# Attention of layers 1 and 3 in a fused four-layer transformer: scores on four 32-row groups, keys not expanded, rotary partners by transfers

## The reference, cut to what matters

```python
# layer 1
qkv = h @ w_qkv + b_qkv
q = _rope(q.reshape(B, T, n_head, hd)); k = _rope(k.reshape(B, T, n_head, hd))
attn = softmax(einsum('bhqd,bhkd->bhqk', q, k) * (1.0 / np.sqrt(hd)))
out = einsum('bhqk,bhkd->bhqd', attn, v)
x = x + (out.reshape(B, T, C) @ w_ao + b_ao)
# _rope: o0 = x0*cos - x1*sin ; o1 = x1*cos + x0*sin   (x0, x1: even and odd features)
# layer 3: no _rope; padding mask of keys and queries; x = x + gate * (out @ proj_w.T + proj_b)
```

## Time and profile before

| | us |
|---|---|
| median of three runs | 2149.85 |
| the profiled execution, its own time | 2150.09 |
| span of the profile | 2148.3 |
| mean granted TensorE clock | 0.993 |
| PE, DVE, ACT, POOL busy | 2049.8, 1314.9, 987.4, 405.0 |

### The profile page before, as it was taken

One profiled execution on the slowest core, in us unless ns is written; L12 is line 12 of the kernel. 1 busy time (PEld: TensorE's weight loads), 2 busy tenths in 40 slices (PEclk: granted clock), 3 DMA queues, 4 the chain that ended last, 5 costly groups with the idle time before them and its releaser, 6 DMA issues.

```text
span 2148.3 us, 44435 instructions
## 1 busy us (share of the span) xinstructions
PE 2049.8 (95%) x15652; PEld 1670.8 (78%) x15652; DVE 1314.9 (61%) x2537; ACT 987.4 (46%) x1581; POOL 405.0 (19%) x381
## 2 busy tenths in 40 slices
PE   7999999999999999999999999998999999998998
PEld 6887887778777888877777777776888777787887
DVE  5856565767766565654444555456666677775664
ACT  3444555444444333334444444445444555454443
POOL 3632112223221010101111111112001222210000
PEclk9999999999999999999999999999999999999999
DMA  6000000000000000000000000000000000000000
GB/s 224 21 10 8 7 11 15 9 7 15 7 8 13 18 20 10 20 5 7 7 6 5 5 0 5 5 2 16 5 5 5 16 6 10 10 1 9 21 20 30
DMA packets 18405, 33.38 MB, mean 16 GB/s; under 512 B 1298, under 2 KB 12050, under 8 KB 17810
## 3 DMA queue, kind: packets, MB, share of 16 engines
q1 hardware_dynamic: 18322, 32.25, 4.7%
HBM read 28.06 MB, written 4.19 MB: 15 GB/s over the span
## 4 chain that ended last, share of the span: by engine, by line
PE 79%; DVE 9%; issue 7%; ACT 2%; POOL 2%; DMA 0%; DVEq 0%; SPq 0%; ACTq 0%; POOLq 0%
PE psum L591 21%; PE psum L593 20%; PE psum L592 19%; PE psum L688 4%; PE psum L701 3%; PE psum L633 2%; PE psum L720 2%; PE psum L786 2%; PE psum L734 2%; PE psum L677 1%; DVE xn L1093 1%; PE psum L526 1%; DVE h_lo L1114 1%; DVE pb L1169 1%; PE psum L685 1%
## 5 line engine op out<-in xcount | busy, mean ns | idle before, releaser
L591 PE MATMUL psum<-h_hi,w_lo 128*128 128x512 f32 x1120 | 463.4, 414 | 11.7 <-DVE h_lo L1114 6.3
L593 PE MATMUL psum<-h_hi,w_hi 128*128 128x512 f32 x1120 | 441.6, 394 | 0.0
L592 PE MATMUL psum<-h_lo,w_hi 128*128 128x512 f32 x1120 | 440.8, 394 | 0.0
L1221 DVE TENSOR_TENSOR hid_lo<-hid,hid_hi 128x512 fp32r<-128x512 f32 x256 | 194.0, 759 | 266.2 <-ACT hid_hi L967 265.9
L967 ACT ACTIVATE hid_hi<-hid 128x512 fp32r<-128x512 f32 x256 | 161.7, 632 | 223.1 <-PE psum L593 133.0
L591 PEld LDWEIGHTS psum<-h_hi,w_lo 128*128 128x128 f32 x1120 | 212.4, 190 | 62.4 <-issue 11.0
L593 PEld LDWEIGHTS psum<-h_hi,w_hi 128*128 128x128 f32 x1120 | 211.8, 189 | 49.5
L592 PEld LDWEIGHTS psum<-h_lo,w_hi 128*128 128x128 f32 x1120 | 212.6, 190 | 39.0
L1303 POOL TENSOR_TENSOR rstd<-ms,half_t 128x4 f32<-128x4 f32 x64 | 65.4, 1021 | 903.9 <-DVE ms L1088 485.1
L1166 DVE TENSOR_REDUCE mx<-psum 128x8 f32<-128x512 f32 x192 | 132.4, 690 | 160.0 <-PE psum L677 106.7
L962 ACT ACTIVATE hid<-psum,vec 128x512 f32<-128x512 f32 x192 | 131.8, 687 | 182.8 <-PE psum L593 166.9
(11 more groups left out here) (140 smaller groups left out, 3601.1 us busy)
## 6 DMA issues: line engine op xcount, KB each, us to landing
stage<-in_w_dram SPq DMA_DIRECT2D x24, 256.0 KB, 2.7
stage<-in_w_dram SPq DMA_DIRECT2D x8, 512.0 KB, 3.5
out_dram<-xres SPq DMA_DIRECT2D x8, 512.0 KB, 2.9
xres<-in_x_dram SPq DMA_DIRECT2D x1, 3584.0 KB, 18.4
modw_mod<-in_modw_dram SPq DMA_DIRECT2D x2, 1536.0 KB, 13.6
stage<-in_w_dram SPq DMA_DIRECT2D x8, 384.0 KB, 3.3
stage<-in_w_dram SPq DMA_DIRECT2D x8, 192.0 KB, 2.4
modw_film<-in_modw_dram SPq DMA_DIRECT2D x1, 1024.0 KB, 7.4
```

The costliest lines, as they stand in the source:

```text
L591: nc.tensor.matmul(dst, s_lo, m_hi, start=start and j == 0, stop=False)
L592: nc.tensor.matmul(dst, s_hi, m_lo, start=False, stop=False)
L593: ins = nc.tensor.matmul(dst, s_hi, m_hi, start=False, stop=stop and j == len(pairs) - 1)
L1221: nc.vector.tensor_tensor(hid_lo[:, slot, :], hid32[:, slot, :], hid_hi[:, slot, :].bitcast(F32), ALU.subtract).then_inc(sem["hid"], 1)
```

## The change

1. Scores, layers 1 and 3: the keys stand in `kk` as projected, [128 rows, 512], not expanded. For each sequence four products run on the 32-row groups r = 0..3, each with 128 stationary columns (`qb`) and 64 moving columns, into bank r of four banks. All steps use the same columns of these four banks, so that scores of a step wait for both `s_free`, that is for DVE's pass over the step before. The mask of layer 3 becomes four products of 128 columns.
2. Layer 1: q and k are projected once. ACT writes the rows with bias to `rows1`, two transfers issued by ACT (`q_swap`, `k_swap`) exchange even and odd partitions into `swapped`, DVE multiplies the projection by cos (after ACT's copy), POOL multiplies `swapped` by sin and adds (`q_rot`, `k_rot`). ACT's four copies of keys per projection are gone.
3. `merge`, `proj` and `back` (and `back` of the mlp phases) fill the A banks, two fills each, and free them in halves. The wide banks are left to `heads`, the turned weights and the mlp.
4. Layer 1's `norm` is ACT's, not DVE's.
5. `on` is a stage of its own, and the table has a new order. `UP_AFTER`, the place of the next mlp's first projections, moves too.

```diff
@@ order_of, layers 1 and 3
-        return mask(1, 0) + [own("scores", 0), prev("probs_t", 7), own("q", 1), own("q_out", 1), prev("pv", 6), own("share"),
-                own("scores", 1), own("probs_t", 0), own("v", 0), prev("pv", 7), own("v_out", 0), own("v", 1),
-                own("v_out", 1), nxt("stats"),
-                own("scores", 2), nxt("norm"), own("probs_t", 1), prev("merge"), own("k", 1), own("k_out", 1), own("pv", 0),
...
+        return ([own("scores", 0), prev("probs_t", 7), prev("on", 5)] + [own("mask", 1)] * masks +
+                [own("k_swap", 1), own("q_rot", 1)] * turned + [prev("pv", 6), own("v", 0), prev("pv", 7), own("v_out", 0),
+                 nxt("stats"),
+                 own("scores", 1), own("probs_t", 0), prev("on", 7)] + [own("k_rot", 1)] * turned +
+                [own("v", 1), own("v_out", 1), nxt("norm"), own("share"),
+                 own("scores", 2), own("probs_t", 1), prev("merge"), own("pv", 0), own("q_out", 1), nxt("turn"),
+                 own("scores", 3), own("probs_t", 2), prev("proj"), own("pv", 1), nxt("split"),
+                 own("scores", 4), own("probs_t", 3), own("on", 1), nxt("q", 0), own("pv", 2), prev("back")] +
...
+                [own("scores", 6), own("probs_t", 5), own("on", 3), own("pv", 4), nxt("q", 1), nxt("q_out", 0)] +
...
@@ PE, scores
-                        for g in range(2):
-                            ins = nc.tensor.matmul(dst.rearrange("p (r g k) -> p r g k", g=2, k=S)[:, :, g, :],
-                                                   qb[:, c, 2 * j + g, :, :].rearrange("p h q -> p (h q)"),
-                                                   kx[:, c, 2 * j + g, :, :], start=layer == 1, stop=layer == 1 or g == 1)
+                        wait_alone(pe, sem[f"s_free{1 - slot}"], n_at(f"s_free{1 - slot}", ph, b, (k + 1) // 2))
...
+                            for r in range(4):
+                                rows = slice(32 * r, 32 * r + 32)
+                                ins = nc.tensor.matmul(group_scores[:, r, g * S:(g + 1) * S],
+                                                       qb[rows, c, seq, :, :].rearrange("p h q -> p (h q)"),
+                                                       kk[rows, c, seq * S:(seq + 1) * S], start=layer == 1,
+                                                       stop=layer == 1 or g == 1)
@@ PE, merge
-                    for g in range(SEQ):
-                        ins = nc.tensor.transpose(wide[:, g // 4, (g % 4) * P:(g % 4 + 1) * P], on[:, g, :], ident)
-                    ins.then_inc(sem["w_full"], 1)
+                    for u in range(2):
+                        dst, full = fill_a(ph, s, k, b, u)
+                        for g in range(4):
+                            ins = nc.tensor.transpose(dst[:, g * P:(g + 1) * P], on[:, 4 * u + g, :], ident)
+                        ins.then_inc(full, 1)
@@ ACT, new: normalizing, and the rotary partners of layer 1
+                elif s == "norm" and PHASES[ph] == ("attn", 1):
+                    act.wait_ge(sem["rstd"], n_at("rstd", ph, b, 1))
+                    for t in range(TILES):
+                        ins = nc.scalar.activation(xn[:, t, :], xres[:, b * TILES + t, :], ACT.Copy, scale=rstd[:, t:t + 1])
+                    for odd in range(2):
+                        act.dma_start(swapped[odd:P:2, which, :],
+                                      rows1[1 - odd:P:2, which, :]).then_inc(sem[f"{name}_swapped"], 16)
@@ DVE, heads' outputs: own stage
-                elif s == "pv" and layer in (1, 3):
-                    if slot == 0:
-                        return
+                elif s == "on":
                     dve.wait_ge(sem["o_full"], n_at("o_full", ph, b, k + 1))
```

More of the change, by code:

```diff
@@ L102, in order_of @@
     if layer in (1, 3):
-        mask = (lambda c, off: [("mask", c, off)]) if layer == 3 else (lambda c, off: [])
-        return mask(1, 0) + [own("scores", 0), prev("probs_t", 7), own("q", 1), own("q_out", 1), prev("pv", 6), own("share"),
-                own("scores", 1), own("probs_t", 0), own("v", 0), prev("pv", 7), own("v_out", 0), own("v", 1),
-                own("v_out", 1), nxt("stats"),
-                own("scores", 2), nxt("norm"), own("probs_t", 1), prev("merge"), own("k", 1), own("k_out", 1), own("pv", 0),
[L108 to L112, removed]
+        masks = layer == 3
@@ L139, in fills_in @@
         return DC
+    if s in ("merge", "proj", "back") and (kind == "mlp" or layer in (1, 3)):
+        return 2
     if kind == "attn" and s in ("q", "k", "v"):
-        return 2 if layer == 1 and s != "v" else 1
+        return 1
     return 1 if kind == "attn" and layer == 2 and s == "probs_t" else 0
@@ L284, in build @@
         kk = place("kk", [P, DC, BLK], F32, free + 8192)
[L285 to L289, removed]
+        q32 = place("q32", [P, DC, BLK], F32, free + 12288)
+        vb = place("vb", [P, TILES, 2, 2 * PAIRS * HW], F32, free + 16384)
+        on = place("on", [P, SEQ, P], F32, free + 16384 + 8704)
+        rows1 = place("rows1", [P, 2, BLK], F32, rot_at)
+        swapped = place("swapped", [P, 2, BLK], F32, rot_at + 4096)
+        assert free + 16384 + 8704 + 4096 <= wb
         free3 = wa + 8 * 2048
@@ L620, in stage_of @@
                         pe.wait_ge(mod_dve, 6)
-                if is_first(b) and (s, k) in (("probs_t", 0), ("pv", 0), ("down", 0)):
+                if is_first(b) and (s, k) == ("down", 0):
                     pe.wait_ge(sem["x_done"], n_at("x_done", ph, 0, 1))
+                if is_first(b) and (s, k) == ("probs_t", 0) and layer in (1, 3):
+                    pe.wait_ge(sem["out_rows"], n_at("out_rows", ph, 0, 0))
+                if is_first(b) and (s, k) == ("up", 0):
+                    for sl in range(2):
+                        pe.wait_ge(sem[f"s_free{sl}"], n_at(f"s_free{sl}", ph, 0, 0))
                 if s == "split" and ph == 0 and is_first(b):
@@ L779, in stage_of @@
                     pe.wait_ge(sem["out_rows"], n_at("out_rows", ph, b, 2))
-                    if kind == "mlp":
-                        pe.wait_ge(sem["x_done"], n_at("x_done", ph, b, 1))
-                    dst = mlp_back if kind == "mlp" else wide
-                    for t in range(TILES):
-                        for m in range(DC):
-                            o = (t % 2) * D + m * P
-                            ins = nc.tensor.transpose(dst[:, t // 2, o:o + P], y[:, m, t * P:(t + 1) * P], ident)
-                    ins.then_inc(sem["back" if kind == "mlp" else "w_full"], 1)
+                    for u in range(2):
+                        if layer == 2 and kind == "attn":
+                            dst, full = wide[:, u, :], sem["w_full"]
+                        else:
+                            dst, full = fill_a(ph, s, k, b, u)
+                        for t in range(2):
+                            for m in range(DC):
+                                o, tile = t * D + m * P, 2 * u + t
+                                ins = nc.tensor.transpose(dst[:, o:o + P], y[:, m, tile * P:(tile + 1) * P], ident)
+                        if u == 1 or full is not sem["w_full"]:
+                            ins.then_inc(full, 1)
             pe.wait_ge(sem["x_done"], n_at("x_done", 0, 0, 1))
@@ L1232, in stage_of @@
                     for m in range(DC):
[L1233 to L1246 removed]
+                        src = wide[:, m, :]
```

267 lines of the change are left out of this document (151 added, 116 removed).

## The result

The changed kernel takes 2270.23 us (median of four runs, 2262.48 to 2273.02), the kernel before 2148.95: 1.0559 times as long, 95% interval 1.0530 to 1.0587. The forecast was +58 us, the measurement +121. The direction was right, the time lies above the range, which ended at 2256. One of the eight executions of on_early (experiment 1) took 3219.51 us at a mean granted clock of 0.555, where the other seven took 2148.70 to 2153.41; the ratios leave it out, and its cause isn't known.

What follows compares the result with a forecast made beforehand. PE was taken to bound both attention stages. New waits and clock loss less PE savings gave +2.3 us a block in layer 1 and +5.4 in layer 3; 7.5 x 7.7 = +58 on 2150.09 gave 2208 us, range 2142 to 2256.

Steps and rivals of the forecast that it cites:

- Work taken off PE: Projections and scores on PE: 5.5 and 2.1 us a block saved in layer 1, 2.7 in layer 3.
- the change of tile shape: Score groups on PE: 0.14 us added to 0.46 for switching tile shape, giving 0.6 us in layer 1.
- The waits behind: PE's pv 4, 6 and 2 wait for VectorE's `on`: 2.9, 3.2, 0.9 us in layer 1; 2 x 2.3 + 0.9 in layer 3.
- Merge and turn in the projection banks: Turn waits until ScalarE and VectorE have read the merge: 3.6 us a block in layer 1, 2.4 in layer 3.
- h: Projection of q waits for h_lo: 1.3 us a block in layer 1, 0.6 in layer 3.
- Transfers hidden: Rotary transfers in layer 1: key ready 6.3 us after its projection, PE needs 9.5 us to scores 0, so no cost.
- The clock: Layers 1 and 3: one low-clock stretch in every second block, costing 0.8 us a block.
- the ends of the stages: Ramp and end of each attention stage count as a half block less, giving the factor 7.5 on the per-block change.
- Rival (c): Clock falls more than once a block in layers 1 and 3: 36 us more, 2244 us; chance 0.25.
- The range: Whole kernel: 2142 to 2256 us, leaving out rivals of total chance 0.15.

Runs made afterwards that it cites:

- on_early, experiment 1: Changed kernel with each `on` moved right behind the product it divides, ahead of the next pass over the scores; 2152.55 us, 1.0017 times the kernel before.
- added_wide: on_early with two products of 512 columns added ahead of each group of scores in layers 1 and 3; 2165.84 us, 1.0086 times the kernel before.
- experiment 2, before_on_late: Kernel before with only `on` moved late, behind the pass of a later segment; 2241.54 us, 1.0441 times the kernel before.
- Experiments 4 to 6: Changed kernel with scores over all 128 rows, 2454.99 us; on_early with score products made twice, 2191.42 us, or with two 512-column products per score group, 2165.84 us.
- one_wide: on_early with stages reordered per layer, plus one unread 512-column product ahead of every score group in layers 1 and 3; 2148.75 us, 1.0000 times the kernel before.
- held: on_early with stages reordered per layer, plus unread products (10 of 224 columns, 4 of 512) in two waits a block; 2121.82 us, 0.9885 times the kernel before.
- full_rows: Changed kernel with each of the eight score products of a group taken over all 128 rows in place of 32; 2454.99 us, 1.1436 times the kernel before.
- experiment 3: Changed kernel with unread products filling PE's waits before the fourth and sixth weight-times-value products and before turn; 2203.61 us, 1.0265 times the kernel before.

## Why the prediction was wrong, by its steps

- *Work taken off PE*: right. A group of scores takes 0.60 us in layer 1 from its start to the turns (525.85 to 526.45), the value taken between the bounds 0.3 and 1.84; taking the row groups away gave 1.83, the upper bound. That it was met to the digit is in part luck, since the 0.14 for the change of tile shape had no row behind it. In layer 3 it takes 0.62 with the mask, where the forecast had 0.75: 3.8 us saved a block for 2.7. The whole saving can be had from added_wide, whose clock is full: its span is 14.5 us over before, with 59 us of added products, 34 us more idle time and 2 us more lost to the clock, so about 80 us were saved; the forecast had 7.5 x 10.3 = 77, and with layer 3's 3.8 it is 85.
- *The waits behind* `on`: right. 7.0 us a block in layer 1 (2.9 + 3.2 + 0.9 = 7.0 forecast), 5.0 in layer 3 (5.5). Their cause is shown by experiment 1, and by 2 from the other side.
- *Merge and turn in the projection banks*: 3.2 us (3.6) and 1.9 (2.4), a little less than said. *h*: 1.3 and 0.7 (1.3 and 0.6).
- *Transfers hidden*: nothing speaks against it. They land after 2.1 us, and none of the 2.0 us that all score groups waited in the whole execution was for the rotary sums:

```profile
L706 PE MATMUL psum<-kk,qb 32*128 32x64 f32 x2048 | 94.9, 307 | 2.0 <-DVEq L1216 1.1 <-issue 0.9
```

- *The clock*: this term failed, by its size. It was 0.8 us a block in both layers. The sum without the clock, with the measured waits and scores, is 38.66 + 11.5 - 1.95 - 7.6 = 40.6 us in layer 1 and 33.25 + 7.6 - 1.2 - 3.8 = 35.85 in layer 3. The measured 49.0 and 40.9 leave 8.4 and 5.0 us. The trace bears this out directly: over the six periods the stretches at 0.50 add up to 17.6 and 8.5 us a block, of which 1.3 and 0.0 fall on waits; half of the rest, 8.2 and 4.3 us, is the work that they cost (the mean clocks of the windows allow 8.8 and 4.9). So the clock took about 8 and 4 to 5 us a block where the forecast had 0.8. Without any clock loss the sums give 7.5 x (1.1 + 2.6) = 28 us over the kernel before; most of the +121 is the clock. Put into the forecast, 8.4 and 5.0 for 0.8 each are 7.5 x (7.6 + 4.2) = +88 us on 2208; the smaller waits and layer 3's quicker scores take back 7.5 x (0.4 + 2.0) = 18: 2278. The four executions took 2262 to 2273; whether the ends of the stages, counted as half a block, make up the difference isn't shown.
- *Rival (c)*, with 2244 us, had the right mechanism at 0.25, and its price was too low as well, for the same reason. I counted stretches by the one in the earlier trace rows, 3.4 us long, and took 1.6 us for each. Here they were up to 10.24 us long inside the blocks, and three a block in layer 1. The error was to carry a price per wait over from a kernel whose work between the waits was wide. The change narrowed that work itself (256-column scores became 64-column ones, and in layer 1 24 products of 512 columns went), so each wait cost more clock than before: experiment 2, with waits of up to 2.2 us beside the old work, had 48 us of low time, on_early 120 with less idle time. The Trainium skill (TensorE: Matmul & The Clock Gate, Why this matters for your kernels) warns only of longer idle gaps between bursts of products. The traces agree that gaps cost clock, but they differ in the length: a gap of 1.4 us (1780.66, on_early) was enough here. Experiments 4 to 6 show the clock to depend on the work beside the gaps too.
- *The range* took its upper end from rival (c), and ended 14 us under the measurement.

Settled: `on` behind the pass costs 118 us, waits and clock together; at equal idle and nearly equal busy time, added wide work held the clock where added narrow work did not. Open: how much each kind of narrow product counts, whether it is their width or their many weight loads, and one_wide's layer 1. Layer 3 never got quicker than before in any of these kernels (33.5 us in held at best). So layer 3 with its old banks and expanded keys beside the new layer 1 is the kernel to try; it wasn't.

## What to carry to other kernels

Where a change takes wide products off TensorE and adds waits, the two are not independent: count the waits, then look at what is left between them, since short waits among narrow products kept the clock at 1.2 GHz here for far longer than they lasted. Read the clock per stage (windows) beside the busy share, since PE's busy time was equal before and after here although it was given some 80 us less to do. A stage that only frees a bank belonged here right behind the work it reads, ahead of the next pass of the same engine (118 us); and where a wait can't be removed, unread wide products in it can pay (17 us in held).

## What the hardware did that I had not expected

- Low-clock stretches outlasted the waits: 10.24 us at 0.50 with PE busy for 9.19 us (changed kernel) or 9.45 (on_early).
- Busy 250.48 of 280 us at a mean clock of 0.82 (full_rows) against busy 232.02 at 0.96 (before_on_late).
- Filling waits with work that nothing reads made a kernel faster: 59 us in experiment 3 (by the spans), 17 us (2138.49 to 2121.82) in held.
- Four row groups of 32 rows: 0.55 us for 16 records (layer 3) against 1.83 over the whole array, 3.3 times.
